# Weights of a shared MLP kept as halves between its two passes, and seven products from the fifth item of the second pass

## The reference, cut to what matters

```python
for e in range(N_SHARED):                       # 2 shared experts, 1024 hidden units each
    h = silu(x_flat @ s_w1[e].T) * (x_flat @ s_w3[e].T)
    shared_out = shared_out + h @ s_w2[e].T
shared_out = shared_out / N_SHARED
...
for e in range(N_EXPERTS):                      # 8 routed experts, 2 chosen per token
    h = gelu(x_flat @ r_w1[e].T)
    routed_out = routed_out + h @ r_w2[e].T * gates_full[:, e:e + 1]
out = (shared_out + routed_out) / (N_SHARED + TOP_K)
```

## Time and profile before

| | before |
|---|---|
| median of 3 runs | 1943.27 us (1942.8 to 1946.58) |
| profiled execution | 1942.84 us |
| its span, first to last instruction | 1941.2 us |
| mean granted clock of TensorE | 0.994 |
| TensorE busy | 1903.2 us, 98% |
| VectorE busy | 1166.6 us, 60% |
| ScalarE busy | 875.2 us, 45% |
| GpSimd busy | 156.5 us, 8% |
| DMA | 314.02 MB, mean 162 GB/s |

### The profile page before, as it was taken

How to read it: one execution, slowest core, us unless ns; L and a number is a source line. 1 busy time by engine, 2 the same in 40 slices (tenths; PEclk the granted TensorE clock), 3 DMA queues, 4 the chain that set the end, 5 groups by cost and what they waited for, 6 DMA issues and landing times. The chain is left out here.

```text
span 1941.2 us, 47321 instructions
## 1 busy us (share of the span) xinstructions
PE 1903.2 (98%) x18980; PEld 1237.5 (64%) x18980; DVE 1166.6 (60%) x2563; ACT 875.2 (45%) x1816; POOL 156.5 (8%) x160
## 2 busy tenths in 40 slices
PE   8999989999999999999999999999999999999997
PEld 7999954444444434444444444457777777899996
DVE  6666645554797655312111116778778886788886
ACT  4444455433122444434333344534444443577775
POOL 0000000000000000221221101111111110000000
PEclk8999999999999999999999999999999999999999
DMA  7033337876354455999998957665454557152332
GB/s 306 14 134 136 131 142 213 224 213 205 112 174 153 166 191 176 192 251 200 229 212 203 202 146 232 198 182 152 128 158 137 158 146 249 46 176 35 48 55 47
DMA packets 305680, 314.02 MB, mean 162 GB/s; under 512 B 228744, under 2 KB 246286, under 8 KB 298575
## 3 DMA queue, kind: packets, MB, share of 16 engines
q1 hardware_dynamic: 292382, 267.53, 47.7%
q0 software_dynamic: 13104, 43.79, 9.7%
HBM read 191.98 MB, written 73.66 MB: 137 GB/s over the span
## 5 line engine op out<-in xcount | busy, mean ns | idle before, releaser
L1255 PE MATMUL sh_p<-xh,arena 128*128 128x512 f16 x1280 | 382.6, 381 | 7.7 <-ACT sh_gated L1530 4.7
L1326 PE MATMUL p<-sh_h_hi,arena 128*128 128x512 f16 x1024 | 304.8, 379 | 1.0 <-DVE sh_h_lo L1905 1.0
L1255 PE MATMUL sh_p<-xl,arena 128*128 128x512 f16 x640 | 243.6, 381 | 0.0
L2265 DVE SCALAR_TENSOR_TENSOR ro_hs<-ro_h,fac,ro_hs 128x512 f16<-128x512 f32 x71 | 53.4, 752 | 297.2 <-ACT ro_hs L2251 297.2
L1255 PEld LDWEIGHTS sh_p<-xh,arena 128*128 128x128 f16 x1280 | 125.1, 98 | 160.5 <-ACT sh_gated L1530 5.2
L2208 PE MATMUL ro_py<-arena,ro_ht 128*128 x852 | 195.0, 379 | 1.9 <-DMA ro_ht<-ro_hs 1.9
L1326 PE MATMUL p<-sh_h_lo,arena 128*128 128x512 f16 x512 | 194.0, 379 | 0.0
L1501 ACT CAST sh_h_hi<-sh_gated 128x512 f16<-128x512 f32 x128 | 79.1, 618 | 234.3 <-DVE sh_gated L1997 207.6
L1326 PEld LDWEIGHTS p<-sh_h_hi,arena 128*128 128x128 f16 x1024 | 96.8, 98 | 107.1 <-DVE sh_h_lo L1905 1.7
L2208 PEld LDWEIGHTS ro_py<-arena,ro_ht 128*128 128x128 f16 x852 | 83.4, 98 | 102.5 <-issue 2.3
L1997 DVE SCALAR_TENSOR_TENSOR sh_gated<-sh_p,fac,sh_gated 128x512 f32<-128x512 f32 x80 | 60.0, 750 | 100.2 <-PE sh_p L1255 99.9
(11 more groups left out here) (329 smaller groups left out, 3919.8 us busy)
## 6 DMA issues: line engine op xcount, KB each, us to landing
stage<-in_shared_w SPq DMA_DIRECT2D x29, 768.0 KB, 5.3
routed_rows<-xres SPq DMA_DIRECT2D x71, 256.0 KB, 2.6
stage<-in_norms_r SPq DMA_DIRECT2D x16, 1024.0 KB, 4.8
stage<-in_routed_w SPq DMA_DIRECT2D x16, 1024.0 KB, 6.3
stage<-in_norms SPq DMA_DIRECT2D x14, 1024.0 KB, 5.0
arena<-x SPq DMA_DIRECT2D x12, 1024.0 KB, 5.6
x<-xres SPq DMA_DIRECT2D x16, 512.0 KB, 2.6
x_rows<-arena SPq DMA_DIRECT2D x8, 1024.0 KB, 8.9
```

Source lines behind the costliest of these rows:

```text
L1255: mm = nc.tensor.matmul(p1[u % P1][:], arena[:, w:w + P], x[slot(gl)][:, :, k, :], start=(j == 0), stop=(j == 3 * KD - 1))
L1326: mm = nc.tensor.matmul(p2[m][:], arena[:, w:w + P], h[n % 2][:], start=(i == 0 and j == 0), stop=(i == HID - 1 and j == 2))
L2265: nc.vector.scalar_tensor_tensor(hs[t % TURNS][:, D:2 * D], h[t % 2], fac[:, 3:4], hs[t % TURNS][:, 0:D], ALU.mult, ALU.subtract).then_inc ...
```

## The change

Part 0 stores the split halves of tiles 4 to 15 in DRAM (`tiles`, 768 KB per tile, one per item from item 26). Part 1 loads and splits only tiles 1 to 3 and fetches the other twelve as halves: `load_whole` writes a tile's place in the arena by three DMAs, two from `tiles` and one from `mixed`, whose block stands where `load_s3` would put it. From item 4 (`FIRST`) on, all items of part 1 use seven products. The input blocks t1, t3, t2 and t4 of the first group are made at its own start, in items 0 to 3 (`FIRST_RAW`, `FIRST_HIGH`, `FIRST_LOW`), as the halves of the other blocks are there already. The first two pairs of mixed weights are asked for in items 0 and 1. In SyncE's order of part 0 the load of the weights to be mixed and the store of the mixed ones change places, and both stand ahead of the load of tiles, norms and routed matrices. With `STAGES` counted from `LOADED`, the two recurrent matrices that the leaky scan needs (1 MB each) are asked for in part 1 right behind the three tiles. The diff, without the lines that only rename or count anew:

```diff
+FIRST = 4
...
-    LOADED = HID if first_part else HID - 1
-    load_tile = lambda q: hidden(q + HID - LOADED)
+    LOADED = HID if first_part else FIRST - 1
+    load_tile = lambda q: hidden(q + part)
...
+            extra_flat = [scratch(3 * KD // 2 * CW, None, F16) for _ in range(2)]
+            extra = [a.rearrange("p (b h k n) -> p b h k n", b=3, h=2, k=KD // 2) for a in extra_flat]
...
+            tile_in = {t: sem(f"tile_in{t}") for t in range(FIRST, HID)}
...
-        plain = lambda n: first_part or n < HID
+        plain = lambda n: first_part or n < FIRST
+        STORE_AT = ROUTE_AT
+        FIRST_RAW, FIRST_HIGH, FIRST_LOW = ((0, 1), (2,), (3,)), ((), (0, 1), (2,), (3,)), ((), (0, 1), (2,), (3,))
...
+            T_ORDER = X_ORDER[3:]
+            first_t1 = scan["wr_hi"][:].rearrange("p k n -> p (k n)")[:, 0:KD * CW].rearrange("p (h k n) -> p h k n", h=2, k=KD // 2)
+            raw_place = extra_flat[1].bitcast(F32).rearrange("p (b k n) -> p b k n", b=3, k=KD // 2)
+            first_raw = {n: raw_place[:, i] for n, i in zip(T_ORDER, (0, 1, 2, 0))}
+            blocks_before = lambda gl: len(T_ORDER) + X_BLOCKS * (gl - 1)
...
-                    e, t = n - HID, hidden(n % HID)
+                    e, t = n - FIRST, hidden(n % HID)
...
+                def store_tile(t):
+                    if t == FIRST:
+                        sp.wait_ge(stage_done, LOADED)
+                    sp.dma_start(dram["tiles"][t - FIRST], arena[:, t * 2 * TILE:(t + 1) * 2 * TILE]).then_inc(tile_stored, 16)
+                def load_whole(t):
+                    halves_of = lambda a: a.rearrange("p (h n) -> p h n", h=2)
+                    place, kept = halves_of(arena[:, t * 2 * TILE:(t + 1) * 2 * TILE]), halves_of(dram["tiles"][t - FIRST])
+                    s3 = halves_of(dram["mixed"][t][:, 4 * QUARTER:6 * QUARTER])
+                    for to, what in ((slice(0, PIECE), kept[:, :, 0:PIECE]), (slice(PIECE, PIECE + QUARTER), s3), (slice(PIECE + QUARTER, TILE), kept[:, :, PIECE + QUARTER:TILE])):
+                        sp.dma_start(place[:, :, to], what).then_inc(tile_in[t], 16)
 
...
+                    if first_part and n in MIX_AT:
+                        load_mix(MIX_AT.index(n))
+                    if first_part and n - 2 in MIX_AT:
+                        store_mix(MIX_AT.index(n - 2))
                     if n + LEAD + 1 < (LOADED if first_part else STAGES):
                         load_stage(n + LEAD + 1)
-                    if first_part and n - 2 in MIX_AT:
-                        store_mix(MIX_AT.index(n - 2))
-                    if first_part and n in MIX_AT:
-                        load_mix(MIX_AT.index(n))
-                    if not first_part and n in (HID - 4, HID - 3):
-                        load_mixed(n + 4)
-                    if not first_part and HID <= n and n + 1 < ITEMS and n > HID:
+                    if first_part and FIRST <= n - STORE_AT + FIRST < HID:
+                        store_tile(n - STORE_AT + FIRST)
+                    if not first_part and n < 2:
+                        load_mixed(n + FIRST)
+                    if not first_part and FIRST < n and n + 1 < ITEMS:
                         load_mixed(n + 1)
-                    if not first_part and 1 <= n <= HID:
+                    if not first_part and n + FIRST < HID:
+                        load_whole(n + FIRST)
+                    if not first_part and 1 <= n <= FIRST:
                         load_s3(n - 1)
...
-                    e, (w, x, (bank_x, bank_y)) = n - HID, operands(n)
-                    if n % HID == 0:
-                        pe.wait_ge(xl_ready, X_BLOCKS * (n // HID))
+                    e, (w, x, (bank_x, bank_y)) = n - FIRST, operands(n)
+                    if n == FIRST or n % HID == 0:
+                        pe.wait_ge(xl_ready, blocks_before(n // HID + 1))
+                    if n < HID:
+                        pe.wait_ge(tile_in[n], 48)
                     if plain(n - 2):
...
-                    if e in (0, HID // 2):
-                        pe.wait_ge(s3_in[e // (HID // 2)], 16 * (HID // 2))
+                    if n == HID:
+                        pe.wait_ge(s3_in, 16 * FIRST)
...
-                    elif n and (first_part or n < HID - 1):
+                    elif n and (first_part or n < FIRST - 1):
...
+                def first_high(r):
+                    raw, high, _ = x_block(0, T_ORDER[r])
+                    act.wait_ge(t_raw, r + 1)
+                    nc.scalar.activation(high, raw, ACT.Copy, scale=scl[:, 0:1]).then_inc(xh_ready, 1)
...
+                    if not first_part and n < len(FIRST_HIGH):
+                        for r in FIRST_HIGH[n]:
+                            first_high(r)
...
+                def first_raw_block(r):
+                    b11, b12, b21, b22 = (quarter_of(xres[slot(0)], n) for n in ("b11", "b12", "b21", "b22"))
+                    if r >= 2:
+                        dve.wait_ge(t_raw, r)
+                    if r == 3:
+                        dve.wait_ge(xl_ready, 1)
+                    name, a, b = (("t1", b12, b11), ("t3", b22, b12), ("t2", b22, first_raw["t1"]), ("t4", b21, first_raw["t2"]))[r]
+                    nc.vector.tensor_tensor(first_raw[name], a, b, ALU.subtract).then_inc(t_raw, 1)
+                def first_low(r):
+                    raw, high, low = x_block(0, T_ORDER[r])
+                    dve.wait_ge(xh_ready, r + 1)
+                    nc.vector.scalar_tensor_tensor(low, raw, scl[:, 0:1], high, ALU.mult, ALU.subtract).then_inc(xl_ready, 1)
...
+                    if not first_part and n < len(FIRST_LOW):
+                        for r in FIRST_LOW[n]:
+                            first_low(r)
+                    if not first_part and n < len(FIRST_RAW):
+                        for r in FIRST_RAW[n]:
+                            first_raw_block(r)
...
+            "tiles": nc.dram_tensor("tiles", (HID - FIRST, P, 2 * TILE), F16, kind="Internal").ap(),
```

More of the change, by code:

```diff
@@ L1034, in x_block @@
                     return [quarter_of(t, name) for t in (slot_x, high, low)]
+                raw = raw_t[name] if gl else first_raw[name]
                 if name == "t1":
-                    return [raw_t[name], quarter_of(high, "b12"), quarter_of(low, "b12")]
+                    return [raw, quarter_of(high, "b12"), quarter_of(low, "b12")] if gl else [raw, first_t1[:, 0], first_t1[:, 1]]
                 more = extra[gl % 2][:, ("t2", "t3", "t4").index(name)]
-                return [raw_t[name], more[:, 0], more[:, 1]]
+                return [raw, more[:, 0], more[:, 1]]
         tile_cols = lambda b, j: b[:, j // 2, :, (j % 2) * P:(j % 2) * P + P]
@@ L1102, in load_s3 @@
                     place = arena[:, w0:w0 + 2 * TILE].rearrange("p (h n) -> p h n", h=2)[:, :, PIECE:PIECE + QUARTER]
-                    sp.dma_start(place, dram["mixed"][hidden(i)][:, 4 * QUARTER:6 * QUARTER].rearrange("p (h n) -> p h n", h=2)).then_inc(s3_in[i // (HID // 2)], 16)
+                    sp.dma_start(place, dram["mixed"][hidden(i)][:, 4 * QUARTER:6 * QUARTER].rearrange("p (h n) -> p h n", h=2)).then_inc(s3_in, 16)
+                def store_tile(t):
[8 more added lines that the diff above has]
+                        sp.dma_start(place[:, :, to], what).then_inc(tile_in[t], 16)
                 def turn_look(a, k):
@@ L1227, in _ @@
                     sp.wait_ge(mix_stored, 16 * HID)
+                    sp.wait_ge(tile_stored, 16 * (HID - FIRST))
                 else:
@@ L1237, in first @@
                         pe.wait_ge(xl_ready, KD * (gl + 1 - part))
-                    if gl == 0 and n and n + LOADED >= HID:
-                        pe.wait_ge(stage_done, n + LOADED - HID + 1)
+                    if gl == 0 and n:
+                        pe.wait_ge(stage_done, n + 1 - part)
                     w0 = hidden(i) * 2 * TILE
@@ L1531, in _ @@
                     else:
-                        if n > HID:
+                        if n > FIRST:
                             gate_right(n - 1)
                         keep_p1(n)
-                        if n > HID:
+                        if n > FIRST:
                             high_h(n - 1)
@@ L1542, in _ @@
                         split_tile(n + AHEAD)
+                    if not first_part and n < len(FIRST_HIGH):
+                        for r in FIRST_HIGH[n]:
+                            first_high(r)
                     if not first_part and i in BLOCK_AT and gl + 1 < PART_GROUPS:
+                        if n < HID and BLOCK_AT.index(i) == 0:
+                            act.wait_ge(xl_ready, len(T_ORDER))
                         split_block(gl + 1, BLOCK_AT.index(i))
@@ L1870, in low_block @@
                     raw, high, low = x_block(gl, X_ORDER[b])
-                    dve.wait_ge(xh_ready, X_BLOCKS * (gl - 1) + b + 1)
+                    dve.wait_ge(xh_ready, blocks_before(gl) + b + 1)
```

(6 more changed lines are left out.)

25 lines of the change are left out of this document (13 added, 12 removed).

## The result

| | before | after |
|---|---|---|
| median of the 10 runs of the comparison | 1943.03 us | 1950.09 us (1945.94 to 1952.0) |
| ratio, 95% interval | | 1.003 [1.0022, 1.0038] |
| profiled execution | 1942.84 us | 1951.26 us |
| its span | 1941.2 us | 1949.5 us |
| mean granted clock of TensorE | 0.994 | 0.989 |

The changed kernel is slower by 7.1 us in the medians and 8.3 us in the profiled spans, though TensorE has less to do. First TensorE's timeline of the changed kernel (start, us, engine, line; the idle time before a row in brackets): the first matmul of the second half, the second products of items 1, 3 and 4 with the stop between, and the one other wait of the first group.

A forecast was written before the change was run, and what follows sets the result against it. TensorE was taken as the bound: -7.2 (removed work) - 0.6 (waits) + 10.1 (stop at item 4) + 2.8 (slow clock) = +5.1 us, giving 1948.4 us; own range 1944.5 to 1951.0, chance 0.62.

The forecast's parts named there:

- The place and the releaser: Second half, item 4: TensorE stops at 1185 until VectorE's low part of t4, VectorE having waited 4.5 us for turned rows.
- the bytes ahead: SyncE's queue before the first turn: 2.88 MB more at 374 GB/s take 7.7 us, less 3.2 idle, leaving 4.5 us.
- Rival A: First turn of the second half not delayed, running beside the loads: stop 5.7 us, sum +0.7, 1944.0 us; chance 0.14.
- The size: TensorE's stop at item 4 of the second half: +10.1 us, lower bound +5.7, upper bound +15.0.
- the gathers behind the turn: Start of the second half: two 256 KB gathers, 1.4 us, share the DMA engines with the backlog; half counted, 0.7 us.
- rival C: Whole tiles' short pieces move slowly, at 173 GB/s: stop at item 4 of 15.0 us, sum +10.0, 1953.3 us; chance 0.07.
- The removed work: Second half, items 4 to 15 of the first group: twelve items go from 7.77 to 7.17 us, -7.2 us.
- The waits in items 16 to 20: Second half: the 0.37 us wait at item 16 and two smaller ones behind it go, -0.6 us (0 to -0.9).
- The clock: After the stop at item 4, TensorE's granted clock falls to 0.5 of full speed: +2.8 us.
- Rival D: Items 5 to 13 of the second half: whole-tile loads make mixed weights late, +4.6 us more, 1953.0 us; chance 0.06.
- Rival B: First half: the stop at 692 and its slow clock go, -7.5 us, sum -2.4, 1940.9 us; chance 0.11.
- The stores of the first half: Twelve stores of 768 KB on SyncE's queue from item 26: cost 0, up to +1 if a load of norms slips.

The follow-up runs named there:

- the 60 matmuls: Changed kernel with 60 matmuls of 128x512, whose result nobody reads, ahead of TensorE's wait at item 4: 1946.65 us, 1.0017 of before.
- the last two kernels: Changed kernel with recurrent matrices asked for in items 12 and 13 and input blocks first, 1939.16 us; the same with gathers behind turns of three groups, 1934.56 us.
- both cures: Changed kernel with the recurrent matrices asked for in items 12 and 13 and the input blocks ahead of the turned rows on VectorE: 1939.16 us, 0.9978 of before.

## Why the prediction was right

The forecast was 1948.4 us and the measured median is 1950.09, near the upper end of the own range (1944.5 to 1951.0).

**The place and the releaser** were as forecast: TensorE behind the first products of item 3, let go by the low half of t4, VectorE waiting for the turned rows before that. Moving either of the two things that the step named (the bytes ahead of the turn, VectorE's order) shortened the stop: to 4.43 us where 4.5 were expected, and to 6.99 where 6.9 were, both expected from rows of the changed kernel. **Rival A** is refuted by the 9.16 us that VectorE waited for the turned rows. The stop that it gave for VectorE's order alone, 5.7 us, came out at 4.43, since VectorE was ready 23.15 us after the first matmul of the half, not 24.2 (1183.5 less 1159.3).

**The size** was short by 3.6 us, and the term at fault is the 0.7 us for "the gathers behind the turn". Without them the working has the rows 27.9 us after the first matmul of the half (1182.7 + 4.5, less 1159.3); with the gathers held back they came after 28.05. So the bytes ahead at 374 GB/s were right, short pieces and all: rival C is refuted. With the gathers beside the turn it was 32.40: they cost 4.35 us, not 0.7. Each of these two is one execution; in the kernels with the 60 matmuls and with SyncE's old order, whose DMAs in this place are the same, the rows came after 30.70 and 30.82 us, so the term lies between 2.7 and 4.4. The gathers cost this only together with the longer queue. In the kernel before they were asked for 0.25 us behind the turn, but none of their packets had moved by 1181.5, and the turn landed after 4.3 us, at 1182.6. With the matrices later they were asked for 0.24 us behind it, and it landed after 3.1 us. The longer queue pushed the turn into them. The Trainium skill, page "DMA: Bandwidth & Descriptors", section "Queues, rings and completion order", says that a DMA engine takes turns between the queues that have work, a packet at a time; the trace agrees in that the turn and the gathers, on two queues, both landed late when they met (12.6 against 8.1 us, 9.8 against 6.3). Why the rate falls so low meanwhile, no run shows.

**The removed work** was right (7.17 us per item but for item 11, whose 9.02 us are over the 7.3 that the prediction set as a sign of being wrong; the wait of 1.67 us is the cause, not the work). The waits in items 16 to 20 were worth 2.2 us, outside the bound of 0.9: the wait of 1.02 us in the earlier trace rows went too, and I had counted it as staying. In the kernel with the 60 matmuls item 20 was again 0.5 us longer, so it comes and goes.

**The clock** was right: 2.8 forecast, 2.9 measured, and 2.9 won back when TensorE was kept busy.

**Rival D** came true in one item of nine and once in the last group, 2.7 us together; the wait in item 11 was there in four of the six profiled executions in which the gathers met the turns, and in neither of the two in which they were held back. Since it was missing by itself in two of six, this does not show that the gathers cause it. What the last two kernels show is that holding them back shortens the second half. **Rival B** came true by a part: the stop in the first half shortened but did not vanish, and at 2.84 us it was not nearly as before either.

**Luck.** The stop was 3.6 us over its forecast and the sum no more than that (3.2 us in the profiled executions). That is luck: rivals D and B cancel (+2.7, -2.7), and the waits in items 16 to 20, 1.6 us under the forecast, make up for the scan's +1.2, which was not forecast. The stores of the first half cost nothing: from the second product of item 26 to that of item 51 every distance is what it was.

Left open: why the scan was 1.2 us longer, and which terms make the runs of the changed kernel lie between 1945.94 and 1952.0 us. The profiled executions show the scan, the routed experts, the stop in the first half and the landing of the first turn to vary.

## What to carry to other kernels

When loads are moved ahead of a small transfer that an engine waits for, count the bytes in front of it on its queue, and then ask what it will meet at its new time on the other queues: here the bytes cost 4.5 us by the forecast's working and the meeting 2.7 to 4.4. When work is moved to the start of a step, its whole chain has to be early, the DMA in it too. The cure here was to ask for what nobody needs yet (two matrices) behind that DMA, and to let the engine do first what waits for no DMA.

## What the runs showed of the hardware

A transposing DMA of 256 KB beside two gathers of 256 KB held the DMA engines at 132 GB/s or less in 13 of 14 slices (4.9 us), though for most of that time they were busy; without the gathers the same turn, behind the same queue, held them under 100 GB/s for 1.05 us (the DMA and GB/s rows above). The gathers too landed later, after 9.8 instead of 6.3 us. In the two halves of the shared MLP TensorE's clock fell to 0.5 behind every stop of the profiled executions from 2.48 us up, and behind none of the waits of 1.1 to 1.7 us inside them. The length of a stop alone does not decide it: in the routed experts the clock fell behind stops of 1.98 us (both cures) and 2.28 us (SyncE's old order), but not behind one of 2.32 us (the 60 matmuls), and at the passage from the scan to the first half, where waits of 1.6 and 1.0 us follow each other, it was at 0.5 for 3.4 us in six of the nine profiled executions.
